# GpSimd waits for its own row transfers inside a block, in three stages of a graph network kernel

## The chip, the cores and the metric

The kernel runs on one core of a Trainium2 chip. The metric is the device time of one execution in microseconds; before the change it is 7640.43 us, the median of 3 runs (7639.8 to 7643.08).

## The reference

Four layers of a graph network run one after another on 6250 nodes of 64 features and 206,250 edges, with a layer norm after each:

```python
x = _layernorm(x + L0(x, edge_weight, edge_weight_n2, ..., src, dst))   # two weighted sums of neighbours
x = _layernorm(x + L1(x, edge_index, edge_attr_32, ...))   # sum, max, mean of edge attributes by src
x = _layernorm(x + L2(x, edge_index, ...))                 # gaussian mixture convolution
x = _layernorm(x + L3(x, edge_index, edge_attr_32, ...))   # messages per edge, then a GRU
```

Layer 0 needs, for each node, the sum over its incoming edges of weight times the features of the source node, for two sets of weights. Layer 1 needs the edge attributes grouped by source node.

## The kernel before, in words

The edges, sorted by destination, are cut into 51 blocks (NBK) of 4096: 128 partitions times 32 columns (CB). An edge's row is 36 words, 144 bytes (RW): 32 attributes, destination, two weights, source.

**First pass (`placing`).** VectorE works out, for each edge of a block, a place in HBM, and GpSimd writes the block's rows there with 32 indirect transfers, one per column, each of 128 rows (line 321, to `pay_d`). The first edge of each source node in a block goes to a grid of 49 x 128 cells, any others to a list behind it. Two blocks later the grid is read back as a whole, and VectorE (lines 514 to 519) and TensorE (lines 415 to 419) turn it into layer 0's sums. The stage's order is written out by hand. `over_thirds` unrolls three blocks, since rows, places and grids have three buffers, with a semaphore `rows_out[j]` for each. In one stage VectorE does, for block b: `hots` (lines 450 to 457), then `open_grid` of block b-2 (lines 500 to 509), and seven steps of `messages` of block b-2, among which stand `ranks(b)` (ahead of step 3) and `places(b)` (ahead of step 5), whose last line, 497, lets GpSimd start on block b. A step's messages wait until TensorE is through with those of two steps earlier. TensorE does the counts and lookups of block b first, and then the seven steps of block b-2.

SyncE's queue is in order. For block b it loads the broadcast row `lo_row` (line 299) once `hots` of the previous block are done, waits for the rows of block b-3 to have landed, loads the rows of block b (line 302), fills the block's grid and list in HBM (lines 304 and 305), and then, once block b-2's rows have landed, reads back the grid of block b-2 (line 293).

**Layer 0's list (`layer0_rest`).** Edges not in a grid are worked through in 51 blocks of 10 columns (SC). SyncE loads a block's rows (line 652) and clears a part of two other arrays (lines 654 and 655); GpSimd gathers the source nodes' features with 10 indirect transfers (line 672, to `r_x`); VectorE multiplies them with the weights (lines 741 and 743), which frees the row buffer for SyncE three blocks on, and TensorE sums. Three buffers.

**Layer 1's scatter (`layer1_scatter`).** The same 51 blocks are written to their sorted places: 10 indirect transfers per block (line 1091, to `sorted_d`), once VectorE has worked out the places (line 1207). The places need the row of the next block, which is loaded when the block two before has landed.

GpSimd does nothing but the indirect transfers in these three stages. It issues one after another and waits for none inside a block.

Of the kernel before, what the change touches and what calls it, by code (L numbers as in the profile page):

```python
# [5 lines left out]
CB = 32  # L6
BE = P * CB
SC = 10
# [56 lines left out]
def over_thirds(eng, blocks, body):  # L65
    for b in range(3):
        body(b, 0, b)
    with eng.Fori(1, blocks // 3) as i:
        for j in range(3):
            body(i * 3 + j, i, j)  # L70
# [152 lines left out]
def placing(nc, z, k, a):  # L223
    NT, NBK, HC = z.NT, z.NBK, CB // 2
    BK = 8
    with ExitStack() as ctx:
# [38 lines left out]
        rows_out = [sem(f"rows_out{j}") for j in range(3)]  # L265
# [19 lines left out]
        with nc.Block() as block:  # L285
            @block.sync
            def _(sp):
                def load_grid(b, i, j):
                    sp.wait_ge(rows_out[j], i * (CB * 16) + CB * 16)
                    sp.sem_inc(starts, 1)  # L290
                    sp.wait_ge(grid_used, b + 1)
                    sp.sem_inc(starts, 1)
                    sp.dma_start(grid[j][:, :, :].rearrange("p s w -> p (s w)"),
                                 gv[at(b)].rearrange("b l w -> (b l) w")).then_inc(grid_in[j], 16)

                def stage(b, i, j):
                    wait(sp, lo_hot_ready, b)
                    sp.sem_inc(starts, 1)
                    sp.dma_start(lo_row[:, :], a["lo_d"][at(b), :].to_broadcast([P, BE])).then_inc(lo_in, 16)
                    wait(sp, rows_out[j], i * (CB * 16))  # L300
                    sp.sem_inc(starts, 1)
                    sp.dma_start(row[j][:, :, :].rearrange("p c w -> p (c w)"),
                                 a["pay"][at(b)].rearrange("b p w -> (b p) w")).then_inc(row_in[j], 16)
                    sp.dma_start(gv[at(b)].rearrange("b l w -> (b l) w"), fg).then_inc(filled[j], 16)
                    sp.dma_start(sv[at(b)].rearrange("b p w -> (b p) w"), fs).then_inc(filled[j], 16)
                    two_back(load_grid, b, i, j)

                over_thirds(sp, NBK, stage)
                load_grid(NBK - 2, NBK // 3 - 1, 1)
                load_grid(NBK - 1, NBK // 3 - 1, 2)  # L310
                sp.wait_ge(starts, 4 * NBK)

            @block.gpsimd
            def _(pool):
                def stage(b, i, j):
                    pool.wait_ge(filled[j], i * 32 + 32)
                    pool.wait_ge(row_in[j], i * 16 + 16)
                    pool.wait_ge(place_ready, b + 1)
                    pool.sem_inc(k.pool_steps, 1)
                    for c in range(CB):  # L320
                        pool.indirect_dma_start(a["pay_d"][:, :], bass.IndirectOffsetOnAxis(ap=place[j][:, c:c + 1], axis=0),  # L321
                                                row[j][:, c, :], None).then_inc(rows_out[j], 16)

                over_thirds(pool, NBK, stage)
# [245 lines left out]
def over_rounds(eng, z, k, body):  # L570
    thirds = z.NBK // 3
    rounds = n_rounds(eng, k)
    with eng.Fori(0, rounds) as r:
        with eng.Fori(0, thirds // 2) as i:
            for h in range(2):
                for j in range(3):
                    body(r * z.NBK + i * 6 + (h * 3 + j), r * thirds + i * 2 + h, i * 6 + (h * 3 + j), j, r)
        for m in range(thirds - thirds % 2, thirds):
            for j in range(3):
                body(r * z.NBK + (m * 3 + j), r * thirds + m, m * 3 + j, j, r)  # L580
# [32 lines left out]
def layer0_rest(nc, z, k, a):  # L613
    NBK = z.NBK
    with ExitStack() as ctx:
# [24 lines left out]
        x_in = [sem(f"r0_x_in{j}") for j in range(3)]  # L640
# [3 lines left out]
        with nc.Block() as block:  # L644
            @block.sync
            def _(sp):
                sp.dma_start(deg[:, :], a["deg_w_d"].rearrange("(a n) -> a n", a=1)).then_inc(deg_in, 16)

                def body(n, m, b, j, r):
                    sp.wait_ge(free, n + 1)  # L650
                    sp.sem_inc(k.sync_steps, 1)
                    sp.dma_start(row[j][:, :, :].rearrange("p c w -> p (c w)"),
                                 sv[bass.ds(b * NR + r, 1)].rearrange("k p w -> (k p) w")).then_inc(row_in[j], 16)
                    sp.dma_start(zv[at(b)], a["none"], max_dma_last_dim=1024).then_inc(cleared, 16)
                    sp.dma_start(dv[at(b)], a["far"]).then_inc(cleared, 16)

                over_rounds(sp, z, k, body)
                sp.dma_start(a["drel_d"][NR * NBK].rearrange("p s -> (p s)"), a["far"][0, 0:P * z.NT]).then_inc(cleared, 16)
                rounds = n_rounds(sp, k)
                sp.wait_ge(cleared, rounds * (NBK * 32) + 16)  # L660
                sp.sem_inc(k.sync_steps, 1)
                sp.wait_ge(deg_done, 1)
                sp.dma_start(a["deg_d"].rearrange("(a n) -> a n", a=1), deg[:, 0:z.NP]).then_inc(deg_out, 16)
                sp.wait_ge(deg_out, 16)

            @block.gpsimd
            def _(pool):
                def body(n, m, b, j, r):
                    pool.wait_ge(row_in[j], m * 16 + 16)
                    pool.sem_inc(k.pool_steps, 1)  # L670
                    for c in range(SC):
                        pool.indirect_dma_start(xs[j][:, c, :], None, a["x"][:, :],  # L672
                                                bass.IndirectOffsetOnAxis(ap=row[j][:, c, AT_SRC:AT_SRC + 1].bitcast(i32), axis=0)
                                                ).then_inc(x_in[j], 16)

                over_rounds(pool, z, k, body)
# [326 lines left out]
def scan_pairs(eng, z, k):  # L1003
    return eng.value_load(k.counts_i[0:1, 2:3], min_val=1, max_val=z.pairs)
# [7 lines left out]
def layer1_scatter(nc, z, k, a):  # L1012
    NT = z.NT
    with ExitStack() as ctx:
# [25 lines left out]
        rows_out = [sem(f"s_rows_out{j}") for j in range(3)]  # L1040
# [6 lines left out]
        with nc.Block() as block:  # L1047
            @block.sync
            def _(sp):
                sp.wait_ge(nothing_set, 1)  # L1050

                pairs = scan_pairs(sp, z, k)

                def clear(j):
                    for q in range(4):
                        sp.dma_start(quarter(a["sorted_d"], z, pairs, q, j), nothing[:, :]).then_inc(cleared, 16)

                for j in range(3):
                    clear(j)
                with sp.Fori(0, pairs) as i:  # L1060
                    clear(i * 2 + 3)
                    clear(i * 2 + 4)

                def load(at_row, m, j):
                    sp.wait_ge(rows_out[j], m * (SC * 16) + 16)
                    sp.sem_inc(k.sync_steps, 1)
                    sp.dma_start(row[j][:, :, :].rearrange("p c w -> p (c w)"),
                                 sv[bass.ds(at_row, 1)].rearrange("k p w -> (k p) w")).then_inc(row_in[j], 16)

                def body(n, m, b, j, r):  # L1070
                    load(b * NR + r, m, j)

                over_rounds(sp, z, k, body)
                rounds = n_rounds(sp, k)
                load(0, rounds * (z.NBK // 3), 0)

            @block.gpsimd
            def _(pool):
                pool.wait_ge(nothing_set, 1)
                for j in range(3):  # L1080
                    pool.dma_start(a["sorted_d"][z.SR4 + j * SR:z.SR4 + j * SR + P, :],
                                   nothing[:, 0:RW]).then_inc(rows_out[j], 16)
                pairs = scan_pairs(pool, z, k)
                pool.wait_ge(cleared, pairs * 128 + 192)
                pool.sem_inc(k.pool_steps, 1)

                def body(n, m, b, j, r):
                    pool.wait_ge(place_ready, n + 1)
                    pool.sem_inc(k.pool_steps, 1)
                    for c in range(SC):  # L1090
                        pool.indirect_dma_start(a["sorted_d"][:, :], bass.IndirectOffsetOnAxis(ap=place[j][:, c:c + 1], axis=0),  # L1091
                                                row[j][:, c, :], None).then_inc(rows_out[j], 16)

                over_rounds(pool, z, k, body)
                rounds = pool.value_load(k.counts_i[0:1, 0:1], min_val=1, max_val=NR)
                for j in range(3):
                    pool.wait_ge(rows_out[j], rounds * (z.NBK // 3 * SC * 16) + 16)
                    pool.sem_inc(k.pool_steps, 1)
# [1566 lines left out]
```

## Time and profile before

| | us |
|---|---|
| median of 3 runs | 7640.43 |
| span of the profiled execution | 9369.1 |
| GpSimd busy in it | 4789.4 |
| VectorE busy in it | 5345.0 |
| TensorE matmul busy in it | 5537.1 |

The page gives no time beside the span for the profiled execution. The span is 1728.7 us above the median of the runs. An indirect transfer is counted as busy GpSimd time while its descriptors are made; its data moves later. "Idle before" is the time in which the engine stood still ahead of an instruction, with what ended it; "issue" and "remote" mean that the trace shows no cause there.

### The profile page before, as it was taken

How to read it: one execution, taken by the hardware profiler on the slowest of the kernel's cores; microseconds unless marked ns; L12 is line 12 of the kernel's file. 1: busy time of each engine (PE TensorE's matmuls, PEld its weight loads, DVE VectorE, ACT ScalarE, POOL GpSimd, SP SyncE). 2: the span in 40 equal slices, each digit the busy share in tenths (PEclk: the TensorE clock that was granted, in tenths of full speed). 3: DMA queues.
4: the chain of work that ended last, by engine and by line, in shares of the span. 5: the costliest groups of instructions: out<-in, count | busy, mean ns of one | idle time of the engine just before them, and what ended most of it. 6: DMA issues, size and time to landing. Idle time of an engine off the chain costs nothing. (4 is left out here: it accounts for less than half of the span.)

```text
span 9369.1 us, 138875 instructions
## 1 busy us (share of the span) xinstructions
PE 5537.1 (59%) x49076; PEld 4542.6 (48%) x49077; DVE 5345.0 (57%) x9166; ACT 1663.2 (18%) x3235; POOL 4789.4 (51%) x4394
## 2 busy tenths in 40 slices
PE   2555555555555523233455542899996677777777
PEld 1333333333333322223345441899995566666665
DVE  5555655565556533334344455666665677777773
ACT  0111111111111100002111131000002333333333
POOL 3555555555555454550355551455550577667670
PEclk7666676666666666665666675999996788888885
DMA  3222222221222154441100030111110333333330
GB/s 98 77 82 78 73 75 81 78 78 70 81 78 80 40 92 89 88 88 29 42 20 19 20 109 12 26 26 27 27 27 17 106 100 97 95 93 95 95 92 13
DMA packets 392774, 612.74 MB, mean 65 GB/s; under 512 B 158383, under 2 KB 318995, under 8 KB 377363
## 3 DMA queue, kind: packets, MB, share of 16 engines
q1 hardware_dynamic: 240826, 478.03, 16.7%
q0 software_dynamic: 141056, 124.52, 6.4%
q8 instruction: 313, 5.13, 0.2%
q10 hardware_dynamic: 10454, 4.04, 0.2%
q14 instruction: 125, 1.02, 0.0%
HBM read 531.52 MB, written 216.25 MB: 80 GB/s over the span
## 5 line engine op out<-in xcount | busy, mean ns | idle before, releaser
L321 POOL DMA_INDIRECT pay_d<-row,place x1632 | 1719.7, 1054 | 1524.9 <-DVE place L497 947.9
L415 PE MATMUL win<-onehot,val 128*128 128x128 f32 x4998 | 1045.4, 353 | 672.4 <-issue 455.3
L415 PEld LDWEIGHTS win<-onehot,val 128*128 128x128 f32 x4998 | 872.3, 251 | 926.8 <-issue 644.4
L514 DVE TENSOR_TENSOR onehot<-near_dve,drel 128x896 f32<-128x896 f32 x357 | 389.3, 1091 | 1182.2 <-remote 1057.4
L2113 POOL DMA_INDIRECT m_from_src<-from_src_d,m_row x510 | 684.0, 1341 | 628.5 <-issue 375.4
L1712 PE MATMUL g_win<-g_hot,y_part 128*128 128x128 bf16 x14994 | 880.7, 220 | 145.1 <-DVE g_hot L1761 101.1
L1692 POOL DMA_INDIRECT g_x<-xg_d,g_row x510 | 641.5, 1258 | 625.1 <-PE g_win L1712 411.7
L1712 PEld LDWEIGHTS g_win<-g_hot,y_part 128*128 128x128 bf16 x14994 | 857.3, 99 | 166.8 <-DVE g_hot L1761 102.1
L1091 POOL DMA_INDIRECT sorted_d<-s_row,s_place x510 | 494.1, 969 | 531.0 <-DVE s_place L1207 368.5
L672 POOL DMA_INDIRECT r_x<-in_x,r_row x510 | 485.2, 951 | 500.9 <-DMA r_row<-pay_d 351.2
L2116 POOL DMA_INDIRECT m_from_dst<-from_dst_d,m_row x510 | 631.0, 1237 | 160.0 <-issue 155.7
L390 PE MATMUL pair<-hot_hi,hot_lo 128*128 128x392 bf16 (+3 forms) x1632 | 295.5, 346 | 639.2 <-DVE hot_hi L453 627.6
L337 ACT ACTIVATE hot<-onehot 128x896 bf16<-128x896 f32 x357 | 333.7, 950 | 1728.3 <-DVEq L521 1720.9
L390 PEld LDWEIGHTS pair<-hot_hi,hot_lo 128*128 128x128 bf16 x1632 | 197.3, 127 | 765.4 <-DVE hot_hi L453 375.8
L704 PE MATMUL r_win<-r_onehot,r_val 128*128 128x160 f32 x1020 | 231.6, 395 | 558.7 <-DVEq L731 369.0
L2145 PE MATMUL m_pre<-m_w_four,m_ea_t 96*128 96x192 f32 (+1 forms) x1428 | 487.4, 425 | 117.1 <-ACT m_ea_t L2229 93.1
L704 PEld LDWEIGHTS r_win<-r_onehot,r_val 128*128 128x128 f32 x1020 | 210.6, 265 | 582.7 <-DVEq L731 394.5
L2149 PEld LDWEIGHTS m_pre<-m_q_win,m_hot_t 128*128 128x128 bf16 x7497 | 360.4, 104 | 202.5 <-issue 135.1
L2149 PE MATMUL m_pre<-m_q_win,m_hot_t 128*128 128x64 bf16 x7497 | 395.8, 201 | 96.3 <-issue 94.2
L2285 DVE TENSOR_TENSOR m_hot<-iota,m_drel 128x896 bf16<-128x896 f32 x361 | 391.8, 1086 | 87.8 <-DMA xt<-in_xT 70.8
L2163 PE MATMUL m_win<-m_hot,m_parts 128*128 128x128 bf16 x2499 | 356.2, 232 | 111.9 <-issue 111.3
L1761 DVE TENSOR_TENSOR g_hot<-iota,g_drel 128x896 bf16<-128x896 f32 x364 | 375.0, 1087 | 82.0 <-PE g_win L1712 55.5
(410 smaller groups left out, 11491.4 us busy)
## 6 DMA issues: line engine op xcount, KB each, us to landing
m_hot_t<-drow_d SPq DMA_DIRECT2D x52, 1568.0 KB
scan_d<-in_none SPq DMA_DIRECT2D x51, 1034.2 KB
lo_row<-lo_d SPq DMA_DIRECT2D x51, 1024.0 KB
m_grid<-pay_d SPq DMA_DIRECT2D x52, 882.0 KB
pay_d<-in_fill SPq DMA_DIRECT2D x51, 882.0 KB
grid<-pay_d SPq DMA_DIRECT2D x51, 882.0 KB, 3.8
pay_d<-in_fill SPq DMA_DIRECT2D x51, 720.0 KB
row<-in_pay SPq DMA_DIRECT2D x51, 576.0 KB
```

Source lines behind the costliest of these rows:

```text
L321: pool.indirect_dma_start(a["pay_d"][:, :], bass.IndirectOffsetOnAxis(ap=place[j][:, c:c + 1], axis=0), row[j][:, c, :], None).then_inc(ro ...
L390: last = mm(pair[h][:, q, c * NT:BK * NT].rearrange("p (n s) -> p n s", s=NT), hot_lo[:, e, :], hot_hi[:, e, :].unsqueeze(1).to_broadcast( ...
L415: mm(win[:, :], val[u % 2][:, s, :], onehot[u % 2][:, s, :], start=(u == 0 and s == 0), stop=(u == NS - 1 and s == SUB - 1))
L672: pool.indirect_dma_start(xs[j][:, c, :], None, a["x"][:, :], bass.IndirectOffsetOnAxis(ap=row[j][:, c, AT_SRC:AT_SRC + 1].bitcast(i32), a ...
L704: mm(win[j][:, :], val[j][:, c, :], onehot[j][:, c, :], start=(c == 0), stop=(c == SC - 1))
L1091: pool.indirect_dma_start(a["sorted_d"][:, :], bass.IndirectOffsetOnAxis(ap=place[j][:, c:c + 1], axis=0), row[j][:, c, :], None).then_inc ...
L1692: pool.indirect_dma_start(xs[j][:, c, :], None, a["xg_d"][:, :], bass.IndirectOffsetOnAxis(ap=row[j][:, c, AT_SRC:AT_SRC + 1].bitcast(i32) ...
L1712: last = mm(win[:, h, 0:W], k.y[q][:, t, h * P:(h + 1) * P], hot[u][:, s, :], start=(t == 0 and q == 0), stop=(t == NT - 1 and q == 2))
L2113: pool.indirect_dma_start(ps_x[j][:, c, :], None, a["from_src_d"][:, :], bass.IndirectOffsetOnAxis(ap=row[j][:, c, AT_SRC:AT_SRC + 1].bitc ...
L2116: pool.indirect_dma_start(qs_x[j][:, c, :], None, a["from_dst_d"][:, :], bass.IndirectOffsetOnAxis(ap=row[j][:, c, AT_DST:AT_DST + 1].bitc ...
L2145: mm(out[:, first * D:(first + size) * D], ea_t[u % 2][0:size * F, o:o + P], w_four[0:size * F, 0:size * D], start=True, stop=False)
L2149: last = mm(out[:, s * D:(s + 1) * D], hot_t[j][:, (u * SUB + s) * P:(u * SUB + s + 1) * P], q_win[j][:, q * D:(q + 1) * D], start=False, ...
```

## The change

Inside a block GpSimd now waits until all transfers of this block begun so far have landed: ahead of the columns 8, 16 and 24 of 32 in the first pass, and ahead of column 5 of 10 in the other two stages. After each wait it adds one to a step counter.

```diff
@@ placing, gpsimd
                     for c in range(CB):
+                        if c in (8, 16, 24):
+                            pool.wait_ge(rows_out[j], i * (CB * 16) + c * 16)
+                            pool.sem_inc(k.pool_steps, 1)
                         pool.indirect_dma_start(a["pay_d"][:, :], ...).then_inc(rows_out[j], 16)
@@ layer0_rest, gpsimd
                     for c in range(SC):
+                        if c == SC // 2:
+                            pool.wait_ge(x_in[j], m * (SC * 16) + c * 16)
+                            pool.sem_inc(k.pool_steps, 1)
                         pool.indirect_dma_start(xs[j][:, c, :], ...).then_inc(x_in[j], 16)
@@ layer1_scatter, gpsimd
                     for c in range(SC):
+                        if c == SC // 2:
+                            pool.wait_ge(rows_out[j], m * (SC * 16) + (16 + c * 16))
+                            pool.sem_inc(k.pool_steps, 1)
                         pool.indirect_dma_start(a["sorted_d"][:, :], ...).then_inc(rows_out[j], 16)
```

## Rows read from the trace of the kernel before

**Rows 1.** The page: the costliest groups of GpSimd's three stages.
```profile
L321 POOL DMA_INDIRECT pay_d<-row,place x1632 | 1719.7, 1054 | 1524.9 <-DVE place L497 947.9
...
L1091 POOL DMA_INDIRECT sorted_d<-s_row,s_place x510 | 494.1, 969 | 531.0 <-DVE s_place L1207 368.5
L672 POOL DMA_INDIRECT r_x<-in_x,r_row x510 | 485.2, 951 | 500.9 <-DMA r_row<-pay_d 351.2
```
**Rows 2.** Waits over the span: who waited for what, us in total, times, longest.
```profile
DVE onehot L514 <- remote: 1057.4, 48, 22.9
...
DVE acc L755 <- remote: 460.9, 16, 34.1
...
DVE s_junk L1183 <- remote: 252.3, 17, 18.7
```
**Rows 3.** Windows of the three stages: us, then busy by engine, TensorE's clock, DMA share, GB/s.
```profile
97.00:3270.00 3173.00, 1666.04 (x9160) 1166.40 (x9161) 1807.12 (x2662) 451.68 (x802) 1719.69 (x1632) 0.67 0.21 75
3300.00:4258.00 958.00, 280.07 (x1177) 216.99 (x1178) 347.00 (x588) 76.84 (x50) 485.21 (x510) 0.60 0.49 87
4503.00:5476.00 973.00, 518.56 (x3126) 466.41 (x3124) 428.35 (x1813) 138.81 (x172) 498.26 (x518) 0.66 0.08 21
```
**Rows 4.** Timeline of one block, 2000 to 2083: start, duration, engine, line, [idle before].
```profile
2000.13 0.96 POOL L321 DMA_INDIRECT pay_d<-row,place  x1 [0.30 <-issue]
...
2002.74 0.70 SPq L293 DMA_DIRECT2D grid<-pay_d  x1
...
2006.64 3.36 PE L415 MATMUL win<-onehot,val 128*128 128x128 f32 x14 [0.81 <-DVEq L521]
...
2019.12 0.19 DVE L497 TENSOR_TENSOR place<-away,pos 128x32 int32<-128x32 f32 x1
...
2020.13 0.96 POOL L321 DMA_INDIRECT pay_d<-row,place  x1 [19.03 <-DVE place L497]
...
2038.35 0.18 DVE L501 CAST dst_f<-grid 128x49 f32<-128x49 int32 x1
...
2062.58 0.97 POOL L321 DMA_INDIRECT pay_d<-row,place  x1 [0.30 <-issue]
...
2066.80 1.09 DVE L514 TENSOR_TENSOR onehot<-near_dve,drel 128x896 f32<-128x896 f32 x1 [22.83 <-remote]
...
2082.62 0.96 POOL L321 DMA_INDIRECT pay_d<-row,place  x1 [19.07 <-DVE place L497]
```
**Rows 5.** Timeline of TensorE while VectorE waits for step 0.
```profile
2045.64 0.71 PE L415 MATMUL win<-onehot,val 128*128 128x128 f32 x3
...
2052.08 0.58 PE L418 MATMUL deg<-hot,ones 128*1 128x512 bf16 x1
...
2063.09 0.37 PE L415 MATMUL win<-onehot,val 128*128 128x128 f32 x1 [1.05 <-issue]
2065.19 0.37 PE L415 MATMUL win<-onehot,val 128*128 128x128 f32 x1 [1.73 <-issue]
```
**Rows 6.** Windows: GpSimd's 32 issues of that block, and SyncE's burst of transfers.
```profile
2020.13:2063.55 43.42, 21.15 (x126) 13.84 (x126) 22.13 (x27) 6.16 (x13) 33.96 (x32) 0.70 0.25 89
...
2038.00:2047.00 9.00, 6.92 (x70) 4.71 (x69) 5.58 (x13) 4.26 (x11) 7.17 (x7) 0.83 0.94 364
```
**Rows 7.** Timeline, layer 0's list: its first block, with SyncE's clears.
```profile
3305.75 0.56 SPq L654 DMA_DIRECT2D scan_d<-in_none  x1
...
3311.62 0.95 POOL L672 DMA_INDIRECT r_x<-in_x,r_row  x1 [0.30 <-issue]
...
3321.86 0.82 DVE L741 TENSOR_TENSOR r_val<-r_x,r_near_dve 128x640 f32<-128x640 f32 x1 [21.55 <-DMA r_x<-in_x,r_row]
```
**Rows 8.** Window of three blocks' 30 gathers there.
```profile
3310.85:3348.59 37.74, 11.59 (x48) 8.61 (x48) 7.66 (x11) 3.07 (x2) 28.59 (x31) 0.59 0.84 145
```

**Rows 9.** The page: DMA issues, KB each, median us from issue to landing.
```profile
scan_d<-in_none SPq DMA_DIRECT2D x51, 1034.2 KB
...
grid<-pay_d SPq DMA_DIRECT2D x51, 882.0 KB, 3.8
```

## The prediction

> **What bounds the kernel now.** I read the page's costliest groups first, then the waits, the windows of the three changed stages, and the timeline of one block.
>
> The groups show GpSimd with 1632, 510 and 510 indirect transfers at 0.95 to 1.05 us, and beside each group an idle time about as long as its work: 1524.9, 531.0 and 500.9 us [rows 1]. By these rows GpSimd has room in all three stages. In the first pass it issues its 32 transfers in 43.42 us [rows 6] and then stands for 19.07 us until VectorE has the next places; the block takes 2082.62 - 2020.13 = 62.49 us [rows 4].
>
> But that is the profiled execution, 9369.1 us long, and the timed runs take 7640.43. 1728.7 us of it are not in the time that I must predict, so the first question is where they lie. The waits answer: VectorE stood 1057.4, 460.9 and 252.3 us for "remote", 1770.6 us in all, in the very stages that the change touches [rows 2]. The timeline shows what it stood for: TensorE was at work on step 0, whose matmuls came one by one, 1 to 2 us apart, with no cause shown; it began at 2045.64 and VectorE could go on only at 2066.80 [rows 4, 5]. Elsewhere in the block the same 14 matmuls take 3.36 us [rows 4]. I take this crawl to be of the profiled execution alone. No row proves that; the two sums, 1729 and 1771, are what speaks for it.
>
> Without the crawl the first pass looks different. Step 0 would take TensorE 3.36 us of matmuls and about 1.1 us of degree sums (0.58 and its like), so it would be done at about 2050.1 and not 2066.8: 16.7 us less, 45.8 us a block; at the higher of the clock's two levels the step takes some 2 us less, 43.8 us. I take 45.0. GpSimd's own cycle is 43.42 + 0.30 = 43.7 us. So in the timed runs its idle time per block is not 19 us but about 1.3, and it is as good as the bound.
>
> Layer 0's list: 958 us for 51 blocks, of which 460.9 are crawl, leaves 9.7 us a block [rows 2, 3]; three blocks' gathers, issued without a pause, take 37.74 us, so 12.6 a block [rows 8]. GpSimd is the bound there. Layer 1's scatter: (973 - 252.3) / 51 = 14.1 us a block at most [rows 2, 3]; ten issues take 10 x (0.97 + 0.30) = 12.7 us [rows 1, 4]. It lies between the two; I take 13.4.
>
> As a check: 50 x (62.5 - 45.0) = 875, 958 - 51 x 12.6 = 315 and 973 - 51 x 13.4 = 290 are together 1480 of the 1729 us, and the rest is left for the other two layers.
>
> **What the change adds.** Nothing is removed or moved. It adds 51 x 3 waits in the first pass and 51 x 1 in each of the other stages, 255 in all, each on GpSimd's queue, with the rest of the block's transfers behind it. Who waits for those: SyncE, to read back the grid (line 293) and to load rows; VectorE, for the gathered features (line 741) and for the place buffer three blocks on. The counter increments are register-size work and go with the wait.
>
> *Price of a wait on quiet queues.* GpSimd must see its last transfer land and then start the next. The last issue of a block ended at 2001.09, and SyncE, which waited for its landing, started at 2002.74: 1.65 us for landing and waking up [rows 4]. GpSimd's own waking takes about 0.8 us (places ended at 2019.31, transfer at 2020.13), and SyncE's is in the 1.65. Without the wait the gap is 0.30. So a wait costs 1.65 - 0.30 = 1.35 us. Lower end 1.0, upper 1.8, for the unknown difference between the two engines' waking.
>
> *Price of a wait beside a burst.* Once per block SyncE sends a burst (broadcast row, rows, two fills), and for 9 us the DMA engines are 94% busy at 364 GB/s, 3.3 MB [rows 6]. A row transfer then lands late. The nearest row is in layer 0's list: last gather of the first block issued by 3312.57 behind clears of 1 MB a block (the third was issued at 3305.75), used at 3321.86, 9.3 us later [rows 7, 9]. So one wait costs between 1.35 and 9.0 us. If GpSimd is the bound, SyncE's burst starts when a block's rows have landed, with the grid's read of 0.9 MB in front [rows 9], which is some 2.4 us more at that rate, so it runs from about 2 us to about 13 us of GpSimd's next block; the wait ahead of column 8 begins at about 10 us. It then costs between 1.35 and 4.7; I take 3.35, that is 2.0 more.
>
> The Trainium skill, "DMA: Bandwidth & Descriptors", section "Queues, rings and completion order", says that each DMA engine goes round the queues that have work, packet by packet. By that a small transfer should be held up by single packets only, and every wait would cost 1.35; the total below would be 150 us less. The 9.3 us do not bear it out.
>
> *First pass.* GpSimd's cycle becomes 43.7 + 3 x 1.35 + 2.0 = 49.7 us, and VectorE's is still 45.0. The cover (1.3 us) is gone after the first wait. What is late next is nothing else: from a block's last landing to the places that its grid's read holds up are 1.65 us, 3.8 for the grid's read [rows 9] and some 27 from there to GpSimd's start (2038.35 to 2082.62, less 17 of crawl) [rows 4], about 33 us, and GpSimd spends 50 on the block between. (49.7 - 45.0) x 51 = 240 us. Ends: 43.7 + 3 x 1.0 = 46.7 against 45.8 gives 46 us; 43.7 + 3 x 1.8 + 4.0 = 53.1 against 43.8 gives 474.
>
> *Layer 0's list.* Every wait counts in full. The DMA engines are 84% busy when the gathers run without pause [rows 8], so the wait at column 5 mostly stands beside a clear. Clears come once a block, some 4 us after the previous block's gathers end, and the wait begins 6.3 us after that. Between 1.35 and 9.0; I take 3.2, nearer to the low end since one block's clear and not three is under way. 3.2 x 51 = 163 us (69 to 300).
>
> *Layer 1's scatter.* The DMA engines are 8% busy [rows 3], so the quiet price: 12.7 + 1.35 = 14.05 against 13.4, 0.7 x 51 = 35 us (0 to 70).
>
> **Sum.** 240 + 163 + 35 = 438 us. Made against the profiled execution the same change would be small in the first pass (19 us of idle time cover 6), some 0 to 200 us of 9369 in all; the time asked for is that of the runs, 7640 + 440 = 8080 us.
>
> **Rivals.**
> *A. The idle time is real: no change.* If the crawl were in the timed runs too, or if GpSimd's issues are themselves slower under the profiler (say 1.0 us instead of 1.27, 32 us a block), the waits are covered in the first pass, and the two short stages pay little: 0 to 150 us, 7640 to 7790. For it: the rows as they stand, 19.07 us idle per block. Against it: then the 1729 us must lie elsewhere, and nothing else in the waits is that large.
> *B. Bursts cost what the worst row shows.* Three waits per block in the first pass and the list's wait all meet traffic: 8250 to 8400. For it: 9.3 us in rows 7. Against it: the burst is 9 us of a 45 us block, so two of three waits lie outside.
> *C. Faster.* With the row transfers held back, SyncE's bursts and row loads have the DMA engines to themselves. In layer 0's list GpSimd stood 351.2 us for rows to arrive [rows 1]; if the timed runs keep a third of that, and waits in the middle of the block let the rows through ahead of the gathers, the list would gain up to 120 us while the first pass, were it covered as in A, loses nothing: about 7570. It decides only if row loads and not issues bound the list. Against it: those waits follow the crawl (VectorE frees the buffers late), not a full queue; three blocks ran without any pause [rows 8].
>
> **Chances.** Forecast 8080 with its own range 7880 to 8280: 0.62. A: 0.20. B: 0.12. C: 0.06. From A 0.11 is within 0.2% (15 us, about what a measurement of this kernel can tell from no change) and 0.09 above it. Faster 0.06, same 0.11, slower 0.83. The 8-in-10 range leaves out the lower half of A with C, and the top of B: 7710 to 8310.
>
> **What would show it.** In the changed kernel's profile GpSimd's transfers at columns 8, 16 and 24 have a wait on their own landing of 1.6 us, one of them more; the list's column 5 has 2 to 5 us. In that execution the first pass keeps most of its length (62 us a block), since its idle time there covers the waits. The forecast is wrong if the timed runs rise by less than 150 us, which would put GpSimd's cycle below VectorE's by more than the waits; or if experiments without the first pass's waits give back less than the other two stages' do.

## The result

| | median, us | lowest to highest | runs |
|---|---|---|---|
| kernel before | 7641.76 | 7639.8 to 7643.59 | 4 |
| changed kernel | 8484.37 | 8477.94 to 8492.43 | 4 |

The changed kernel takes 1.1105 times as long (95% interval 1.1091 to 1.1119), 842.6 us more. The forecast was 8080 us with a range of 7710 to 8310: the sign was right and the size was about half.

The kernel before has two levels, and in every run the level went with the chip: 7633 to 7656 us, or 9211 to 9406 us. The execution whose rows stand ahead of the prediction (span 9369.1) is of the second kind, and its time needs no effect of the profiler: on the chip of e1 the runs without a profile took 9365.75 us in the median and the profiled one 9360.81. Every run of the kernel before beside e1 to e12 was on the high level, every one beside e13 to e18 on the low; there the profiled run of the unchanged kernel (e17) took 7653.89 us with a span of 7652.3. The times in the table are all of the low level, so the changed kernel is read here against e17's trace.

The page of the changed kernel (span 8481.0), its groups that answer to [rows 1]: busy us, mean ns | idle before.

```profile
L324 POOL DMA_INDIRECT pay_d<-row,place x1632 | 1697.5, 1040 | 1061.8 <-issue 561.9 <-DMA pay_d<-row,place 499.9
...
L1100 POOL DMA_INDIRECT sorted_d<-s_row,s_place x510 | 493.9, 968 | 324.8 <-issue 139.6 <-DMA sorted_d<-s_row,s_place 102.0 <-DVE s_place L1216 83.2
...
L678 POOL DMA_INDIRECT r_x<-in_x,r_row x510 | 485.4, 952 | 537.9 <-DMA r_x<-in_x,r_row 357.8 <-issue 139.6 <-DMA r_row<-pay_d 40.6
```

The same groups of the unchanged kernel on the low level (e17).

```profile
L321 POOL DMA_INDIRECT pay_d<-row,place x1632 | 1727.4, 1058 | 614.4 <-issue 588.0 <-DVE place L497 26.4
...
L1091 POOL DMA_INDIRECT sorted_d<-s_row,s_place x510 | 494.1, 969 | 238.3 <-issue 155.1 <-DVE s_place L1207 83.2
L672 POOL DMA_INDIRECT r_x<-in_x,r_row x510 | 485.3, 952 | 195.6 <-issue 153.0 <-DMA r_row<-pay_d 42.7
```

The 255 waits on GpSimd's own transfers took 499.9 + 357.8 + 102.0 = 959.7 us. In e17 GpSimd stands in the first pass only 26.4 us for VectorE's places (947.9 in [rows 1]): it is the bound there, and nothing covers a wait.

Windows of the three stages that answer to [rows 3]: first the changed kernel, then e17 (us, busy of PE, PEld, DVE, ACT, POOL, clock, DMA share, GB/s).

```profile
95.00:2762.00 2667.00, 1419.90 (x9150) 1046.60 (x9150) 1810.71 (x2650) 461.71 (x800) 1697.26 (x1632) 0.74 0.25 89
2803.00:3785.00 982.00, 296.06 (x1200) 254.90 (x1200) 353.55 (x595) 76.83 (x50) 484.66 (x510) 0.63 0.39 85
4040.00:4775.00 735.00, 442.06 (x3005) 408.02 (x3003) 409.50 (x1764) 128.79 (x152) 493.41 (x510) 0.73 0.10 25
```

```profile
97.00:2345.00 2248.00, 1321.63 (x9150) 968.57 (x9150) 1801.95 (x2650) 450.99 (x800) 1727.29 (x1632) 0.77 0.30 106
2385.00:3026.00 641.00, 282.87 (x1200) 242.80 (x1200) 355.99 (x597) 76.83 (x50) 485.29 (x510) 0.69 0.69 131
3280.00:3930.00 650.00, 437.28 (x3008) 403.77 (x3006) 414.82 (x1768) 129.19 (x152) 494.10 (x510) 0.77 0.12 29
```

Each stage has the same work in it and is longer: 419, 341 and 85 us, 845 in all. All of the loss is in the three changed stages.

One block of the changed kernel's first pass. Its first row transfer, column 0, starts at 1728.36 and its eighth, column 7, at 1737.25 (timeline: start, duration; in brackets the idle time before). It answers to [rows 4].

```profile
1728.36 0.96 POOL L324 DMA_INDIRECT pay_d<-row,place  x1 [0.30 <-issue]
1729.46 0.34 SPq L293 DMA_DIRECT2D grid<-pay_d  x1
...
1732.44 0.52 SPq L305 DMA_DIRECT2D pay_d<-in_fill  x1
...
1737.25 0.97 POOL L324 DMA_INDIRECT pay_d<-row,place  x1 [0.31 <-issue]
1743.85 0.97 POOL L324 DMA_INDIRECT pay_d<-row,place  x1 [5.63 <-DMA pay_d<-row,place]
```

The gap at column 8 is 5.63 us; 8 and 16 columns later it is 2.01 and 2.03. Windows of the changed kernel beside that gap, with the same columns as above: what the DMA engines do (share and GB/s, last two).

```profile
1729.00:1738.00 9.00, 2.35 (x42) 1.74 (x40) 3.11 (x10) 1.01 (x3) 6.87 (x8) 0.69 1.01 379
...
1740.00:1741.00 1.00, 1.00 (x7) 1.00 (x5) 0.13 (x1) 0.81 (x1) 0.00 (x0) 0.50 0.44 188
1741.00:1742.00 1.00, 1.00 (x4) 0.09 (x2) 0.00 (x0) 0.14 (x1) 0.00 (x0) 0.50 0.17 50
1742.00:1743.00 1.00, 1.00 (x5) 0.94 (x5) 0.83 (x1) 0.00 (x0) 0.00 (x0) 0.50 0.01 3
```

SyncE's burst keeps the engines full for 9 us and is drained at about 1741.7; GpSimd goes on only 2.1 us after that. The wait lasts until the burst is through, and then for about as long as a gap on quiet queues, 2.00 us.

Layer 0's list in the changed kernel (timeline, answers to [rows 7]): the first of the two clears goes out 2.2 us before the wait begins at 3315.71.

```profile
3313.48 0.56 SPq L657 DMA_DIRECT2D scan_d<-in_none  x1
...
3314.24 0.91 SPq L658 DMA_DIRECT2D drel_d<-in_far  x1
3314.76 0.95 POOL L678 DMA_INDIRECT r_x<-in_x,r_row  x1 [0.30 <-issue]
3322.81 0.95 POOL L678 DMA_INDIRECT r_x<-in_x,r_row  x1 [7.10 <-DMA r_x<-in_x,r_row]
```

Its DMA engines over that gap.

```profile
3316.00:3318.00 2.00, 2.00 (x10) 2.00 (x9) 1.62 (x5) 0.10 (x1) 0.00 (x0) 0.50 1.10 287
3318.00:3320.00 2.00, 2.00 (x9) 1.88 (x8) 1.73 (x4) 0.00 (x0) 0.00 (x0) 0.50 1.09 224
3320.00:3321.00 1.00, 1.00 (x6) 0.25 (x4) 0.39 (x3) 0.00 (x0) 0.00 (x0) 0.81 0.35 84
3321.00:3322.00 1.00, 0.12 (x2) 0.00 (x0) 0.00 (x0) 0.00 (x0) 0.00 (x0) 1.00 0.00 0
```

The same picture: full until 3320, idle soon after, GpSimd at 3322.81.

### The profile page after: what moved, and what is told of

Its sections match the earlier page's. It is cut to its first block and busy times, and to the rows that moved or that the text cites. A ratio compares the mean times of both kernels' runs of the same rounds, so it can differ in the third digit from the quotient of the medians.

```text
span 8481.0 us, 139212 instructions
## 1 busy us (share of the span) xinstructions
PE 5116.5 (60%) x49076; PEld 4356.4 (51%) x49077; DVE 5344.4 (63%) x9166; ACT 1671.6 (20%) x3235; POOL 4861.2 (57%) x4394
## 5 line engine op out<-in xcount | busy, mean ns | idle before, releaser
L324 POOL DMA_INDIRECT pay_d<-row,place x1632 | 1697.5, 1040 | 1061.8 <-issue 561.9
L418 PE MATMUL win<-onehot,val 128*128 128x128 f32 x4998 | 833.2, 332 | 490.6 <-DVEq L524 487.7
L418 PEld LDWEIGHTS win<-onehot,val 128*128 128x128 f32 x4998 | 755.4, 238 | 639.0 <-DVEq L524 511.5
L1701 POOL DMA_INDIRECT g_x<-xg_d,g_row x510 | 663.7, 1301 | 560.0 <-PE g_win L1721 324.0
L2122 POOL DMA_INDIRECT m_from_src<-from_src_d,m_row x510 | 661.6, 1297 | 404.8 <-issue 401.7
L2125 POOL DMA_INDIRECT m_from_dst<-from_dst_d,m_row x510 | 725.3, 1422 | 155.5 <-issue 151.0
L678 POOL DMA_INDIRECT r_x<-in_x,r_row x510 | 485.4, 952 | 537.9 <-DMA r_x<-in_x,r_row 357.8
L710 PE MATMUL r_win<-r_onehot,r_val 128*128 128x160 f32 x1020 | 262.1, 446 | 707.4 <-DVEq L737 707.4
L710 PEld LDWEIGHTS r_win<-r_onehot,r_val 128*128 128x128 f32 x1020 | 247.5, 310 | 725.2 <-DVEq L737 725.2
L2175 PE MATMUL m_win<-m_hot,m_parts 128*128 128x128 bf16 x2499 | 334.3, 229 | 205.4 <-DVE m_parts L2312 205.3
L2172 PE MATMUL m_win<-m_hot,m_parts 128*128 128x128 bf16 x2499 | 341.1, 229 | 116.7 <-issue 116.7
L1138 PE MATMUL key_bc<-ident,s_keys 128*128 128x128 f32 x1040 | 229.2, 414 | 270.8 <-ACT s_keys L1115 270.8
```

The source lines that it names most:

```text
L418: mm(win[:, :], val[u % 2][:, s, :], onehot[u % 2][:, s, :], start=(u == 0 and s == 0), stop=(u == NS - 1 and s == SUB - 1))
L710: mm(win[j][:, :], val[j][:, c, :], onehot[j][:, c, :], start=(c == 0), stop=(c == SC - 1))
L1701: pool.indirect_dma_start(xs[j][:, c, :], None, a["xg_d"][:, :], bass.IndirectOffsetOnAxis(ap=row[j][:, c, AT_SRC:AT_SRC + 1].bitcast(i32) ...
L2122: pool.indirect_dma_start(ps_x[j][:, c, :], None, a["from_src_d"][:, :], bass.IndirectOffsetOnAxis(ap=row[j][:, c, AT_SRC:AT_SRC + 1].bitc ...
L2125: pool.indirect_dma_start(qs_x[j][:, c, :], None, a["from_dst_d"][:, :], bass.IndirectOffsetOnAxis(ap=row[j][:, c, AT_DST:AT_DST + 1].bitc ...
```

## The experiments

The table gives the mean length of a block in each stage and the mean gap on GpSimd ahead of each waited column, both worked out from the starts of GpSimd's transfers. The step from one column to the next without a wait leaves a gap of 0.30 us. A dash stands for a column without a wait. "High" and "low" are the level of the kernel before on that run's chip.

| kernel, level | first pass | gap 8 / 16 / 24 | list | gap | scatter | gap |
|---|---|---|---|---|---|---|
| e17 unchanged, low | 44.06 | | 12.56 | | 12.74 | |
| changed, low | 52.36 | 5.74 / 2.06 / 2.00 | 19.34 | 7.01 | 14.43 | 2.00 |
| e18, low | 49.12 | 5.84 | 12.60 | | 12.77 | |
| e13, low | 45.55 | – / 2.00 | 12.57 | | 12.73 | |
| e14, low | 45.54 | – / 2.00 | 13.47 | 1.19 | 14.41 | 1.99 |
| e15, low | 44.05 | | 12.56 | | 12.74 | |
| e16, low | 48.42 | 2.19 / 2.08 / 2.02 | 14.85 | 2.87 | 14.43 | 2.00 |
| e1 unchanged, high | 62.02 | | 18.40 | | 18.83 | |
| e2, high | 53.34 | 6.55 / 2.03 / 2.00 | 18.40 | | 18.68 | |
| e3, high | 62.07 | | 19.93 | 7.60 | 18.62 | |
| e4, high | 62.11 | | 18.40 | | 16.03 | 2.00 |
| e5 changed, high | 53.34 | 6.50 / 2.03 / 2.00 | 19.90 | 7.57 | 15.16 | 2.00 |
| e6, high | 61.95 | | 18.20 | | 18.18 | |
| e7, high | 63.36 | 2.13 | | | | |
| e8, high | 55.11 | – / – / 2.00 | | | | |
| e9, high | 62.07 | | 15.33 | | 18.92 | |
| e10, high | 53.56 | 6.61 / 2.00 / 2.00 | 19.88 | 7.52 | 16.14 | 2.02 |
| e11, high | 53.36 | | 14.76 | 2.79 | 16.81 | |
| e12, high | 62.21 | | 16.61 | 1.87 | 18.77 | |

### The stages one by one (e1 to e4)

e1 is the kernel before, unchanged. e2 has the waits in the first pass alone, e3 in the list alone, e4 in the scatter alone:

```diff
e2 +                        if c in (8, 16, 24):
e2 +                            pool.wait_ge(rows_out[j], i * (CB * 16) + c * 16)
e3 +                            pool.wait_ge(x_in[j], m * (SC * 16) + c * 16)
e4 +                            pool.wait_ge(rows_out[j], m * (SC * 16) + (16 + c * 16))
```

> The kernel before, unchanged, profiled once more. Theory (the crawl of TensorE belongs to that one profiled execution): a span near 7640 us with no wait for 'remote' of 20 us, GpSimd's block in the first pass 43.7 to 45 us apart, in the list 12.6, in the scatter 12.7 to 13.4. Rival (the crawl comes with every profile of this kernel): a span near 9370 us again, blocks 62 us apart.

> Only the first pass's three waits. Theory (GpSimd was the bound before, and every wait costs in full): the block goes to 52.4 us as in the changed kernel, 8.0 to 8.7 us more than before, +410 to +440 us. Rival (VectorE's cycle of 45 us and more covered part): +240 to +380 us, the rest of the 843 us then being the other stages'.

> Only the wait in layer 0's list. Theory (GpSimd bound, one wait of 7.0 us in place of a gap of 0.3): 51 x 6.7 = +342 us. Rival (the stage was bound by something slower than GpSimd's 12.6 us before, so part is covered): +163 us, as in my forecast, or less.

> Only the wait in layer 1's scatter. Theory (GpSimd bound, wait of 2.0 in place of 0.3): 51 x 1.7 = +87 us. Rival (the stage took 13.4 us a block before): +50 us. If the three stages add up, e2 + e3 + e4 = 843 us within 15.

Measured, beside 9365.75 us (9339.83 to 9373.32) for the kernel before: e1 9360.81; e2 8926.64, ratio 0.9533 (0.9511 to 0.9555); e3 9416.64, 1.0051 (1.0036 to 1.0067); e4 9248.02, 0.9884 (0.9863 to 0.9905). These runs fell on the high level, where two of the three edits gain. e1 is timed and shown at that level, which ends the forecast's reading that the crawl belongs to one profiled execution. The edits add up otherwise than on the low level: the first pass loses 8.7 us a block, the scatter 2.8, and only the list gains length, 1.5. The waits of e1 that answer to [rows 2]:

```profile
DVE onehot L514 <- remote: 1092.8, 48, 33.4
...
DVE acc L755 <- remote: 461.3, 16, 34.2
```

Those of e2: the wait for step 0 is no longer among its 20 largest, and the list's stays.

```profile
DVE dst_f L504 <- DMA grid<-pay_d: 552.7, 47, 31.8
POOL pay_d L324 <- DMA pay_d<-row,place: 539.8, 153, 8.3
DVE acc L758 <- remote: 453.4, 16, 29.2
```

GpSimd's waits cost 539.8 us, and the block is still 8.7 us shorter, because VectorE no longer stands some 23 us for step 0.

### The wait or the counter, and which wait (e5 to e8)

e5 is the changed kernel again. e6 keeps the counter's increments and has no waits. e7 has column 8 alone, e8 column 24 alone:

```diff
e6 +                            pool.sem_inc(k.pool_steps, 1)
e7 +                        if c in (8,):
e8 +                        if c in (24,):
```

> The changed kernel, unaltered, timed beside the kernel before on one chip. The kernel before has now been seen at two levels, 7640 us and 9360 us, each steady. Theory (the crawl of TensorE comes with the chip or the way of recording, and the level belongs to the day's chip): beside a kernel before at 9360 us the changed kernel takes about 9360 - 440 + 50 - 120 = 8860 us, from the three stages tried alone, and its first pass is bound by GpSimd at 53 us a block; beside one at 7640 us it takes 8484 us. Rival (the waits themselves make the crawl go away in all stages): 8484 us also beside 9360.

> The changed kernel's counter increments without its waits. Theory (waits alone cost): the time of the kernel before within 0.3%, gaps at the columns 0.3 us. Rival (an extra instruction between two transfers breaks their overlap on GpSimd's queue): gaps above 0.5 us, up to 1 us of each 2.0 us gap.

> First pass with the wait at column 8 alone. Theory (it stands beside SyncE's burst, which follows the landing of the block before): if GpSimd is the bound before, a gap of 5.7 to 6.5 us and +5.4 us a block, +277 us; where the kernel before crawls, the block falls from 62.4 us to GpSimd's 49 to 50. Rival (the place of the wait does not matter): a gap of about 3.3 us, a third of the three.

> First pass with the wait at column 24 alone. Theory (no burst there): a gap of 2.0 us, +1.7 us a block, +87 us if GpSimd is the bound; where the kernel before crawls, either no change, if the crawl comes from TensorE alone, or, if holding back row transfers is what stops the crawl, a fall as with column 8. Rival (place does not matter): the same time as e7_col8.

Measured, beside 9241.31 us (9211.13 to 9262.12): e5 8731.88, ratio 0.944 (0.9408 to 0.9472); e6 9250.57, 1.0006 (0.9992 to 1.0021); e7 9309.52, 1.0077 (1.0048 to 1.0106); e8 8880.67, 0.9615 (0.9589 to 0.964). The increments cost nothing that can be measured. The same kernel that loses 842.6 us on the low level wins 509.4 on the high one. What counts there is a pause of the row transfers after SyncE's burst: e8's, at column 24, wins 361 us; e7's, at column 8 and ahead of a burst that on this level is issued 18.7 us into the block, loses 68. Its gap, 2.13 us, is also what a wait at column 8 costs where no burst is near. Of VectorE's waits, first e7, then e8:

```profile
DVE onehot L517 <- remote: 958.7, 42, 23.9
```

```profile
DVE onehot L517 <- remote: 362.3, 34, 19.1
```

### Is it TensorE's own work? (e9, e10)

Both leave out most of the window matmuls (five of seven per step in the first pass, eight of ten in the list), so layer 0's sums lack those parts; e10 has the change too.

```diff
-                    for s in range(SUB):
+                    for s in (0, SUB - 1):
...
-                        for c in range(SC):
+                        for c in (0, SC - 1):
```

> The kernel before with most of TensorE's window sums left out: two of seven matmuls per step in the first pass and two of ten in the list, so that its crawl can't set the time there. Theory (without the crawl GpSimd's 43.7 us a block was the bound, or VectorE next to it): the first pass falls from 62 to 43.7 to 44.5 us a block, the list to 12.6, as must have been so in the runs at 7640 us. Rival (VectorE's own cycle was 45 us and more, as in my forecast): 45 to 47 us a block and GpSimd idle for the difference.

> The same cuts in the changed kernel. Theory (the 843 us are the waits' price where nothing covers them): first pass 52 to 53.5 us a block, list 19 to 20, scatter 14.4, together 750 to 850 us above e9_light (the scatter still crawls in e9_light, so its 87 us may be missing or have the other sign). Rival (part of the 843 us came from elsewhere than these stages): under 700 us.

Measured, beside 9382.62 us (9366.14 to 9406.02): e9 9215.48, ratio 0.9808 (0.9781 to 0.9835); e10 8855.64, 0.9429 (0.9403 to 0.9455). The first pass is unmoved at 62.07 us a block. Its wait in e9:

```profile
DVE onehot L514 <- remote: 1122.5, 50, 33.4
```

With five of seven matmuls gone VectorE waits for step 0 as long as in e1, until 46.7 us into the block in both, some 3 us after GpSimd's last row transfer (43.4). And it doesn't wait for matmuls that are still to be issued. In a block of e9 that starts at 1956.53 the last matmul of step 0 and that of step 1 are on record long before VectorE goes on (timeline):

```profile
1986.24 0.32 PE L419 MATMUL deg<-hot,ones 128*1 128x384 bf16 x1
...
1989.96 0.53 PE L419 MATMUL deg<-hot,ones 128*1 128x384 bf16 x1
...
2003.22 1.09 DVE L514 TENSOR_TENSOR onehot<-near_dve,drel 128x896 f32<-128x896 f32 x1 [22.83 <-remote]
```

Over 45 blocks VectorE goes on 16.8 us after the end of step 0's record in e9, 11.0 us after it in e1 and 0.04 us after it in e17 (medians). What comes late on the high level is the signal of step 0's end. The ends of matmul records are modelled, so it stays open whether the sums themselves or only their signal is late.

The list is not unmoved. It falls from 18.40 to 15.33 us a block with eight of ten window matmuls gone, about all of the 167 us that e9 is faster: there TensorE's own work is part of the length.

### What makes the list's wait dear (e11, e12)

e11 is e10 with SyncE's clears of `scan_d` and `drel_d` moved behind the list. e12 is the kernel before with a wait for the first two gathers instead of all five, counted on a semaphore of their own:

```diff
e11 +                def clears(n, m, b, j, r):        # the two clears, in an over_rounds of their own
e11 +                over_rounds(sp, z, k, clears)     # after the list's
e12 +                        if c == SC // 2:
e12 +                            pool.wait_ge(x_early[j], m * 32 + 32)
e12 -                                                ).then_inc(x_in[j], 16)
e12 +                                                ).then_inc(x_early[j] if c < 2 else x_in[j], 16)
```

> e10_light_waits with SyncE's clears of 1.1 MB a block moved behind the list's last block. The total says little, since the clears then stand alone at the end. Theory (the list's wait is long because its gathers land behind the clears): the gap at column 5 falls from 7.0 to 7.6 us to 2.0, and the list's block from 19.4 to 14.3. Rival (ten gathers of 256-byte rows are themselves slow to land): the gap stays above 4 us.

> Only the list's wait, but ahead of column 5 GpSimd waits for the first two gathers and not for all five. Theory (the price is the emptied queue plus the burst): on quiet queues the wait would cost nothing (the second gather ended 3.8 us before), beside the clears still 2 to 5 us; gap at column 5 between 2 and 5.5 us against 7.6. Rival (landings come together when a burst ends, so waiting for two is as long as for five): 6.5 to 7.6 us.

One run each: e11 8920.45, e12 9283.44. Without the clears the gap is 2.79 us, not 7.52; so the dear part of the list's wait is the clears. e12's gap is 1.87, but this is no second proof: its clears go out 10.8 us into the block in the median, behind the wait at column 5, where those of e3 go out at 4.0. Even without the clears e11's gap stays 0.8 us above the 2.00 of the other stages; why is not shown.

### The same questions on the low level (e13 to e18)

e13 has column 16 alone; e14 has that, e12's wait in the list and the scatter's wait. e15 takes the burst's fills ahead of the first pass and the clears behind the list, without waits; e16 does so in the changed kernel.

```diff
e13 +                        if c in (16,):
e15 -                    sp.dma_start(gv[at(b)].rearrange("b l w -> (b l) w"), fg).then_inc(filled[j], 16)
e15 -                    sp.dma_start(sv[at(b)].rearrange("b p w -> (b p) w"), fs).then_inc(filled[j], 16)
e15 +                with sp.Fori(0, NBK) as b:        # both fills of all blocks, first
e15 +                pool.wait_ge(filled[0], NBK * 32)
```

> First pass with the wait at column 16 alone. With no wait TensorE's step 0 stands from SyncE's burst until GpSimd's transfers pause (46.7 us into the block), whatever the number of its matmuls. Theory (any pause of GpSimd's transfers behind the burst frees it): here the pause comes about 28 us into the block, step 1 goes on at about 30 to 32, and the block falls to 46 to 50 us, 650 us less beside a kernel before at 9240 to 9380 us. Rival (it is the time that frees it, or two waits are needed): 55 us or more. On a chip where the kernel before takes 7640 us: a gap of 2 to 6 us and 0 to 200 us slower.

> The cheapest set by the runs so far: first pass column 16 alone, list the wait for the first two gathers, scatter as in the changed kernel. Theory: the gains of e13, e12 (100 us) and e4 (118 us) add up, 8400 to 8550 us beside a kernel before at 9240 to 9380, under the changed kernel's 8732 to 8860; beside one at 7640 it would be slower, 7800 to 7950. Rival: the stages' stalls are shared, so that less than 600 us come back.

> The kernel before with SyncE's large transfers out of the loops: all fills of the first pass ahead of its first block, all clears of the list behind its last. That adds some 150 to 350 us at either place, so the blocks are read and not the total. Theory (the stall of TensorE starts with SyncE's burst beside GpSimd's transfers): the first pass falls to 43.7 to 46 us a block and the list to 12.6, which also shows what the blocks take without a stall. Rival (GpSimd's transfers alone stall TensorE): 62 and 18 us a block as before.

> The same in the changed kernel. Theory (a wait costs 1.7 us on quiet queues, the rest is the burst): gaps of 2.0 to 3 us at all columns, 49 to 50 us a block in the first pass and 14.3 to 14.8 in the list; against e15 3 x 1.7 x 51 = 260 us, 51 x 1.9 = 100 us and in the scatter 87 us or a gain of 118, so 240 to 450 us slower than e15. Rival (the gap at column 8 is long for another reason than the burst): 5.5 us and more there.

Measured, beside 7641.81 us (7632.76 to 7652.61): e13 7715.44, ratio 1.0094 (1.0077 to 1.0111); e14 7852.1, 1.0269 (1.0251 to 1.0286); e15 8164.97, 1.0682 (1.0664 to 1.07); e16 8561.79, 1.1195 (1.1176 to 1.1213).

e13's 73.6 us are its first pass: each block is 1.49 us longer, 76 us over the 51. e14 adds 136.7: the scatter's wait 51 x 1.68 = 86, the list's (13.47 - 12.57) x 51 = 46, together 132. e15 is slow because its fills stand alone in front (its first row transfer starts at 341 us, not 97) and its clears alone behind the list (550 us from the list's last block to the scatter's first, not 267), while its blocks keep their length. Between e15 and e16 the 255 waits cost 396.8 us instead of 842.6. By the blocks, the first pass pays 4.37 us and not 8.30, the list 2.29 and not 6.78: (3.93 + 4.49) x 51 = 429 us. So about half of the price in the changed kernel is the meeting of two waits with a burst. GpSimd's groups in e16, whose waits took 318.7 and 146.4 us where the changed kernel has 499.9 and 357.8:

```profile
L326 POOL DMA_INDIRECT pay_d<-row,place x1632 | 1679.4, 1029 | 1130.1 <-issue 811.4 <-DMA pay_d<-row,place 318.7
...
L683 POOL DMA_INDIRECT r_x<-in_x,r_row x510 | 485.1, 951 | 326.7 <-DMA r_x<-in_x,r_row 146.4 <-issue 139.6 <-DMA r_row<-pay_d 40.8
```

e17 is the kernel before and e18 is e7's, on such a chip.

> The kernel before once more, for its trace on a chip where it takes 7640 us, if this is one. Theory (from e13 to e16: GpSimd is the bound in all three stages there): first pass 44.1 us a block with GpSimd idle under 1 us, list 12.56, scatter 12.73, no wait of VectorE for TensorE above 7 us. Rival (VectorE's cycle is the longer, as forecast): 45.0 us a block, GpSimd idle 1.3. On a chip where it takes over 9200 us: the rows of e1 again.

> First pass with the wait at column 8 alone, beside a kernel before at 7640 us. Theory (the burst follows the landing of the block before by 2 us once GpSimd is the bound, so this wait meets it every time): gap 5.7 us, 49.5 us a block, +5.4 x 51 = +277 us. Rival (a lone wait leaves VectorE's order as it was, and the burst comes 18 us into the block, behind column 8, as it did on the other chip): gap 2.0 us, 45.8 us a block, +90 us.

Measured, beside 7649.92 us (7646.51 to 7655.51): e17 7653.89, e18 7903.4, ratio 1.0327 (1.031 to 1.0344). Column 8's wait alone costs 253.5 us of the 842.6, column 16's 73.6. GpSimd's first group in e18 and in e13:

```profile
L324 POOL DMA_INDIRECT pay_d<-row,place x1632 | 1721.7, 1055 | 874.9 <-issue 576.9 <-DMA pay_d<-row,place 298.0
```

```profile
L324 POOL DMA_INDIRECT pay_d<-row,place x1632 | 1718.3, 1053 | 694.8 <-issue 592.3 <-DMA pay_d<-row,place 101.9 <-DVE place L500 0.6
```

The same instruction, eight columns apart, waits 5.84 or 2.00 us, since the burst is drained by column 16. In e17 the burst comes late, where a wait at column 8 would be ahead of it; VectorE's wait for step 0, [rows 4]'s 22.83 us, is 4.70 there, and what ended it is no longer "remote" but TensorE's last matmul of the step (timeline; the block starts with the first line):

```profile
1456.60 0.96 POOL L321 DMA_INDIRECT pay_d<-row,place  x1 [0.74 <-issue]
...
1475.16 0.34 SPq L299 DMA_DIRECT2D lo_row<-lo_d  x1
...
1485.15 1.09 DVE L514 TENSOR_TENSOR onehot<-near_dve,drel 128x896 f32<-128x896 f32 x1 [4.70 <-PE deg L419]
```

As soon as any wait makes GpSimd clearly the bound, VectorE runs ahead, SyncE has only the landing left to wait for, and the burst is issued from 1.1 us into the block in the changed kernel (1729.46), with its first load, `lo_row`, at 2.0 us and not at 18.5. In e18 a block starts at 1526.33, the burst at 1527.60, and column 8's gap ends at 1542.08. The wait at column 8 makes its own collision. The list's does the same: its clears go out 8.8 us into the block in e17 (median), behind column 5, and 3.7 us into it in the changed kernel.

No version beat the kernel before on the low level; e13 comes nearest. On the high level the change itself, e2, e8 and e4 do, and e12 in its one run.

## Why the prediction was wrong

**The step that failed: the price of a wait beside a burst.** The forecast took 3.35 us for column 8 and 3.2 for the list's column 5. They cost 5.74 - 0.30 = 5.44 and 7.01 - 0.30 = 6.71, so 2.09 x 51 = 107 us and 3.51 x 51 = 179 us were missing: 286 of the 405 by which the sum of 438 fell short. Where the two meet was right in both places: SyncE's burst was to run from 2 to 13 us of the block and, in the block shown, runs from 1.1 to 13.3, with the wait from 9.9 (forecast: 10); the clears were to come 4 us after the previous block's last gather and come 4.1 after it. What was wrong is above all what follows the burst. The forecast let column 8's wait end about when the burst does; the traces show the engines drained at 1741.7 and 3320.4, and GpSimd going on 2.1 and 2.4 us later. So column 8's gap is 3.5 us of burst that was left (forecast: 3) and 2.1 behind it, and its price lies even above the forecast's upper end of 4.7. For the list the two ends, 1.35 and 9.0, did hold the value, and the choice within them was made by "one block's clear and not three"; one block's clears alone keep the engines busy for some 6.5 us from their issue (3313.5 to 3320), of which 4.7 were left when the wait began. e11, e16, e7 and e18 with e13 show that it is the bursts: with them gone, past or still to come, the gaps are 2.79 and 2.87 us in the list, 2.19, 2.00 and 2.13 in the first pass.

The Trainium skill, "DMA: Bandwidth & Descriptors", section "Queues, rings and completion order", has each engine go round its queues packet by packet. By the forecast's reading of that, these waits would cost as the quiet ones do. Forecast and runs agree that they do not: 5.44 and 6.71 us beside a burst, 1.89 and 2.57 in e16, where the fills and the clears are away. The forecast put the difference that this reading makes at 150 us; by its own terms it is (2.0 + 1.85) x 51 = 196.

**The quiet price.** 1.35 us was taken, 1.0 to 1.8 allowed; it is 2.00 - 0.30 = 1.70 wherever nothing else moves (first pass, scatter, on both levels). The row taken, SyncE's start 1.65 us after GpSimd's last issue [rows 4], was read as the same as GpSimd's own; GpSimd's is 2.00. Two such waits a block in the first pass and one in the scatter make 3 x 0.35 x 51 = 54 us.

**The bases.** First pass: 45.0 taken, 44.06 in e17, 0.94 x 51 = 48 us. Scatter: 13.4 taken, 12.74 in e17, 34 us. List: 12.6 taken, 12.56. GpSimd was the bound a little more than thought in the first pass and the scatter. The rest takes back about 17 us: GpSimd's own cycle, 52.36 less its three waits' 8.90 = 43.46 against 43.7 us, and the other stages.

| us over 51 blocks | forecast | measured |
|---|---|---|
| first pass | 240 | (52.36 - 44.06) x 51 = 423 |
| list | 163 | (19.34 - 12.56) x 51 = 346 |
| scatter | 35 | (14.43 - 12.74) x 51 = 86 |
| elsewhere | 0 | 842.6 - 855 = -12 |

**What held.** Once the 1729 us that the profiled execution was longer were taken out, GpSimd's queue was the bound in all three stages and the waits showed in full. The reason for taking them out did not hold: the crawl was said to be of the profiled execution alone, and it belongs to the chip. Its place was read rightly: (62.02 - 44.06) x 51 = 916, (18.40 - 12.56) x 51 = 298 and (18.83 - 12.74) x 51 = 311 us, 1525 of the 1707 us between e1 and e17 (forecast: 875 + 315 + 290). In the page the covering idle time is real, but only where the kernel takes 9369 us. One reading of the rows was wrong as well. VectorE was said to stand while TensorE was at work on step 0. But the matmul at 2052.08 in [rows 5], `deg` of line 418, belongs to the end of step 0, so those at 2063.09 and 2065.19 are step 1's, and VectorE went on only at 2066.80. It changed nothing in the sum, since the whole wait was taken out.

**The rivals.** A, the idle time is real: false on the low level, where GpSimd stands 26.4 us for places in the whole first pass. B, every wait meets traffic: its 8250 to 8400 lies nearer to the result than the forecast, but by another way; two of five kinds of wait meet a burst, not all. C, faster: its sign came on the high level, by a cause that it did not name. That the counter costs something: e6 shows nothing (1.0006, 0.9992 to 1.0021).

**The signs named ahead.** Two waits of 1.6 us and a longer one in the first pass: 2.06, 2.00 and 5.74. The list's between 2 and 5: 7.01, outside. The first pass keeping its 62 us a block in the profiled execution: wrong in both ways, 52.36 there and 53.34 on the high level, where the waits didn't only fit in the idle time but ended the wait of VectorE that made it. The last sign was that the first pass's waits, left out, would give back less than the other two stages' do. No run tried that on the low level; by the block lengths it is 423 against 346 + 86 = 432 us, so the sign came, narrowly, and by the list, which costs twice what was forecast.

## What to carry to other kernels

In both places where a wait for GpSimd's own small transfers met large ones, it lasted until those had drained, and then about its quiet price again; add the two, do not take the longer. Look where the large transfers will be once the waiting engine has become the bound, as they move with it. And when a profiled execution and the timed runs are far apart, run the unchanged kernel again before the difference is put down to the profiler.

## What the runs showed of the hardware

The same kernel takes 7653.89 us on one chip and 9360.81 on another, with the same instructions. On the high level VectorE can't go on in the first pass before 46.7 us into the block, though TensorE's records of step 0 end at 35.6 us in e1 and, with most window matmuls left out, at 29.8 us in e9 (medians of 45 blocks). SyncE's burst is issued at 18.5 us and GpSimd's last issue ends at 43.4. On the low level VectorE goes on as soon as the record ends, at 1485.15 - 1456.60 = 28.6 us in the block shown.

Pauses of the row transfers move that point. With one at column 24 (e8) it is 37 to 42 us, with one at column 8 alone, ahead of the burst, 48.0 (e7), and with the changed kernel's, whose burst is early and whose pause is at column 8, about 14 (e5). That a pause behind the burst brings the signal forward is shown by e7 and e8. It is no plain release by the pause, since in e8 GpSimd goes on at 35.2 us and VectorE in the median only at 39.1. That the burst has a part in it is only argued, since e15 ran on the low level alone. Why chips differ stays open.

GpSimd's wait for its own last row transfer, with nothing else under way, made a gap of 2.00 us in the first pass and the scatter, on both levels, against 0.30 between two issues. In the list, to wait for the two gathers begun at columns 0 and 1, ahead of column 5, still made a gap of 1.19 us on the low level (e14), where the clears go out 9.3 us into the block, behind column 5.
